# An LSTM on one Trainium2 core: one more matmul call with a zero operand in each time step

## The reference

```python
xW = einsum('ntd,dk->tnk', x, Wx) + b          # 256 -> 1024 columns
def step(h, c, xw):
    a = xw + h @ Wh                            # [4, 1024]
    i, f, o = sigmoid(a[:, 0:256]), sigmoid(a[:, 256:512]), sigmoid(a[:, 512:768])
    g = tanh(a[:, 768:1024])
    c = f * c + i * g
    h = o * tanh(c)
out = x + hs                                   # h starts as cond_1024, c as 0
```

## Time and profile before

| what | value |
|---|---|
| runs (3) | 1094.28 to 1101.48 us, median 1100.56 us |
| the profiled execution | 1090.95 us |
| its span, first to last instruction | 1089.2 us |
| mean granted clock of TensorE in it | 0.963 of full |
| busy: VectorE, TensorE, ScalarE | 790.8, 697.3, 550.4 us |

### The profile page before, as it was taken

One profiled execution on the slowest core, in us unless ns is written; L12 is line 12 of the kernel. 1 busy time (PEld: TensorE's weight loads), 2 busy tenths in 40 slices (PEclk: granted clock), 3 DMA queues, 4 the chain that ended last, 5 costly groups with the idle time before them and its releaser, 6 DMA issues.

```text
span 1089.2 us, 88137 instructions
## 1 busy us (share of the span) xinstructions
PE 697.3 (64%) x36864; PEld 574.9 (53%) x36864; DVE 790.8 (73%) x4897; ACT 550.4 (51%) x3586; POOL 0.7 (0%) x6
## 2 busy tenths in 40 slices
PE   4666666666666666666666666667666666766664
PEld 3555555555555555555555555555555555545554
DVE  4777777777777777777776777776777777777776
ACT  2455555555545555555554555554545555455554
POOL 0000000000000000000000000000000000000000
PEclk9999999999999999999998999998999998999999
DMA  3000000000000000000000000000000000000000
GB/s 89 5 7 5 6 6 6 6 6 5 7 5 6 7 5 5 6 6 6 6 6 6 5 6 7 5 6 6 6 6 6 6 6 6 5 6 6 6 6 7
DMA packets 32110, 8.74 MB, mean 8 GB/s; under 512 B 31584, under 2 KB 31584, under 8 KB 32096
## 3 DMA queue, kind: packets, MB, share of 16 engines
q1 hardware_dynamic: 31488, 8.41, 3.5%
q10 hardware_dynamic: 608, 0.14, 0.1%
HBM read 6.43 MB, written 2.10 MB: 8 GB/s over the span
## 4 chain that ended last, share of the span: by engine, by line
DVE 51%; PE 24%; ACT 14%; issue 8%; SPq 1%; DVEq 1%; DMA 0%
DVE turned_bank L296 39%; PE gates L364 24%; DVE h_pad L314 8%; ACT tanh_o L212 8%; ACT turned_bank L215 7%; DVE scan_both L301 3%; DVE cell L307 1%; DVEq L330 1%; SPq L139 1%; DVE h_rows L270 0%; DMA wh_raw<-in_L_cond_Wh_dram 0%; SPq L143 0%; DVEq L269 0%; DVE wh L225 0%; DVE wh L222 0%
## 5 line engine op out<-in xcount | busy, mean ns | idle before, releaser
L364 PE MATMUL gates<-wh,h_pad 128*32 128x64 f32 x32768 | 591.2, 227 | 374.8 <-DVE h_pad L314 373.3
L364 PEld LDWEIGHTS gates<-wh,h_pad 128*32 128x32 f32 x32768 | 506.5, 114 | 488.3 <-DVE h_pad L314 486.4
L296 DVE STREAM_TRANSPOSE turned_bank<-gates 128x64 f32<-128x64 f32 x2048 | 478.5, 262 | 182.3 <-PE gates L364 170.0
L203 ACT ACTIVATE tanh_f<-turned_bank 128x8 f32<-128x8 f32 x512 | 90.7, 177 | 438.1 <-DVE turned_bank L296 427.6
L210 ACT ACTIVATE scan_both<-turned_bank 128x8 f32<-128x8 f32 x1024 | 185.1, 181 | 59.9 <-DVE turned_bank L296 17.3
L314 DVE SCALAR_TENSOR_TENSOR h_pad<-tanh_o,turned_bank 128x4 f32<-128x4 f32 x1024 | 132.7, 158 | 74.2 <-ACT turned_bank L215 4.6
L307 DVE TENSOR_TENSOR_SCAN cell<-scan_both 128x12 f32<-128x12 f32 x1024 | 144.0, 181 | 2.1 <-issue 0.3
L215 ACT ACTIVATE turned_bank<-cell 128x4 f32<-128x4 f32 x1024 | 143.3, 172 | 2.5 <-DVE cell L307 0.3
L346 PE MATMUL x_acc<-wx,x_units 128*32 128x128 f32 x2048 | 107.5, 285 | 9.3 <-DVE x_units L249 9.3
L212 ACT ACTIVATE tanh_o<-turned_bank 128x8 f32<-128x8 f32 x512 | 90.7, 177 | 28.9 <-DVE turned_bank L296 6.7
L216 ACT ACTIVATE half_d<-cell 128x8 f32<-128x8 f32 x512 | 100.4, 196 | 0.0
(11 more groups left out here) (24 smaller groups left out, 6.7 us busy)
## 6 DMA issues: line engine op xcount, KB each, us to landing
x_next<-in_x_dram SPq DMA_DIRECT2D x256, 8.0 KB
x_here<-in_x_dram SPq DMA_DIRECT2D x256, 8.0 KB
out_dram<-y_rows SPq DMA_DIRECT2D x256, 8.0 KB
wx_raw<-in_L_cond_Wx_dram SPq DMA_DIRECT2D x8, 128.0 KB, 3.4
wh_raw<-in_L_cond_Wh_dram SPq DMA_DIRECT2D x8, 128.0 KB, 2.7
bias_raw<-in_L_cond_b_dram ACTq DMA_DIRECT2D x4, 32.0 KB, 3.1
h_rows<-in_cond_dram ACTq DMA_DIRECT2D x4, 1.0 KB
```

The costliest lines, as they stand in the source:

```text
L203: nc.scalar.activation(tanh_f[:], of_step(BF, t), ACT.Tanh).then_inc(tanh_f_done, 1)
L296: nc.vector.transpose(turned[k], gates[k][:, 0:W]).then_inc(gates_turned[k], 1)
L364: last = nc.tensor.matmul(gates[k][q * R:(q + 1) * R, 0:W], h_stationary(b, t), wh[:, b, q, columns_of(k)], start=False, stop=b == M - 1, ...
```

## The change

A function `keep_busy` on TensorE issues one call: stationary operand `zeros` (128 rows, 32 columns, all zero), moving operand the 256 columns of `wh[:, 0, 0, :]`, output partitions 0 to 31 of columns 256 to 511 of `x_acc`, which nothing reads. It uses column tile (0, 0) and accumulates (`start=False`). It is called once in each step: right behind the calls for O at t = 0 to 6 (ahead of `x_product` where there is one) and in all steps of the last chunk, and at t = 7 of the loop behind the last `inject`. It carries no wait and raises no semaphore. Two clears are added on VectorE before the loop, of `zeros` and of all 512 columns of `x_acc`, and TensorE waits for `zeroed` to reach 2 ahead of `wx_made` too.

```diff
         h_pad = sb("h_pad", [128, M, (STEPS + 1) * WIN])
+        zeros = sb("zeros", [128, R])
...
             nc.vector.memset(half_d[:], 0.0)
+            nc.vector.memset(zeros[:], 0.0)
+            nc.vector.memset(x_acc[:], 0.0)
...
+            def keep_busy():
+
+                nc.tensor.matmul(x_acc[0:R, GC:2 * GC], zeros[:], wh[:, 0, 0, :], start=False, stop=True,
+                                 tile_position=(0, 0), skip_group_check=True)
+
...
                 for k in (BA, BB, BO):
                     recur(0, k)
                     recur(1, k).then_inc(gates_done[k], 1)
+                if t < STEPS - 1 or not ahead:
+                    keep_busy()
                 if t == STEPS - 1 and ahead:
                     pe.wait_ge(x_part_made, chunk + 2)
                     for k in BANKS:
                         pe.wait_ge(gates_turned[k], now)
                         inject(k)
+                    keep_busy()
                 if ahead and 0 <= t - FIRST_PIECE_AT < len(PIECES):
                     x_product(*PIECES[t - FIRST_PIECE_AT], chunk + 1)
 
+            pe.wait_ge(zeroed, 2)
             pe.wait_ge(wx_made, M)
```

## The result

| | before | changed |
|---|---|---|
| median | 1097.42 us (4 runs, 1087.36 to 1101.48) | 1061.64 us (4 runs, 1060.75 to 1062.23) |
| ratio | | 0.9687, 95% interval 0.9615 to 0.9758 |
| profiled execution | 1090.95 us | 1062.23 us |
| span, mean granted clock | 1089.2 us, 0.963 | 1060.4 us, 0.999 |

The changed kernel is 3% faster, and the forecast of 1068.4 us is 6.8 us too high. Its direction, its range and its mechanism stand; one term of the sum is wrong.

What follows compares the result with a forecast made beforehand. The kernel was taken as one loop of waits, slowed by falls of TensorE's clock. From the profiled 1090.95 us, minus 24.5 for the falls plus 2 at t = 7, gave 1068.4 us; range 1062 to 1085 us.

Steps and rivals of the forecast that it cites:

- What bounds the kernel, and the price of the falls: A loop of waits between engines; falls of TensorE's clock to half cost 24.5 us, about 23 falls.
- Whether the call stops them: The call's 0.43 us lifts TensorE's lean stretches, so the loop's clock falls go: -24.5 us, bounds 0 and -25.3.
- rivals 1, 2 and 4: In order: clock falls as before, 1102.6 us (0.12); falls stay, call overruns, 1117 us (0.04); half go, 1081 us (0.04).
- The call at t = 0 to 6: The call lies in TensorE's idle gap of 0.91 us, or 0.70 us behind an x piece: cost 0.
- The call at t = 7: Behind the last `inject`, the call makes the next step 0.04 us late in 63 trips; taken as 2 us.
- Rival 3: TensorE's sequencer is held up at the loop's end, 7 to 13 us, about 1077 us; chance 0.09 shared with constant part.
- The median and the profiled execution: The median's 9.6 us above the profiled execution is nine more falls, which go too, so the median after is 1068.4 us.
- constant part: The 9.6 us in the median is something other than falls and stays: 1078 us; chance 0.09 shared with the sequencer.
- Before and behind the loop: Both clears, the wait for `zeroed` and the call behind the last step are hidden: 0, or 0.6 us if clears weren't.

## Why the prediction was right, and where it was wrong

- **What bounds the kernel, and the price of the falls.** Right. 23.6 us in the loop were lost to falls, and they are gone. The price from three windows, 0.68 us for 0.001 of clock, was measured as 0.69 on 23 runs (0.73 with the 12 others). One reading behind it was loose: the clock's slices are not "nines and eights from end to end" but nines with three eights, all in the second half. A nine can hide a fall; it is the windows of the trace that show them from 39.5 us on.
- **Whether the call stops them.** Right in its result, and rivals 1, 2 and 4 fall with it: the clock is 0.999, and a call with a zero stationary operand counts (its moving operand isn't zero). The falls came back without the call (clears alone) and stayed away without VectorE's clears, so it is the call. The rule of the Trainium skill ("TensorE: Matmul & The Clock Gate", Part 1) that long idle gaps cost the clock doesn't cover this kernel: the longest of TensorE's 511 waits for `h` before the change took 1.1 us, and the clock fell. What came ahead of a fall was read rightly: three more stretches of 3.4 us that end at a fall, from 36.1, 565.2 and 1036.2 us, have 1.57 us of work too. (That no fall lies behind the stretch from 135.1 is in the trace, where the clock is 1.00 up to 150.44, but not in the rows that the prediction names.) The reasoning by busy time was too cautious: I leaned on the 0.43 us of the call, and 0.11 us did the same. What it is in the call that counts stays open.
- **The call at t = 0 to 6.** Right: 0, and 0 even for two calls.
- **The call at t = 7.** Right: 16.32 against 16.29 us a trip with VectorE's instructions unchanged, and 1.4 us less in the loop without this call, so 1.4 to 2 us where I took 2. Only the call's own column tile is held, and the other tiles start on time. Rival 3 falls: the branches before and after took the same 208 ns, and the next step isn't late by its 0.11 us.
- **The median and the profiled execution.** Borne out: time follows the clock over 35 runs, and no constant part is left. That the 9.6 us between these two were falls is what this leads one to expect; the clocks of the slower runs are not on record.
- **Before and behind the loop.** This is the term that was wrong: "So both clears are hidden: 0". Their time is hidden, but they are two instructions more ahead of VectorE's loop, and that alone saves 6.4 us (1068.04 against 1061.64 us). The sum for the call was 1068.4, and the call by itself measured 1068.0; that it is so close is partly luck, since its terms were uncertain by more than that. The row to read beforehand was VectorE's own: a trip at full clock was 16.29 us where eight steps of 2.016 make 16.13, and I didn't ask what the 0.16 us were. They are 0.12 at t = 4 and 0.04 at t = 6.

## What to carry to other kernels

A chain of short steps can cost TensorE its clock with no long gap anywhere; here the longest wait was 1.1 us. A mean granted clock under 1 and trips of one loop that differ by a fixed amount show it. In this kernel a tiny call of no use in each step (some 0.11 us was enough) gave it back for almost nothing; it costs only where it reaches past the next step's start. When a change adds or removes instructions ahead of an unrolled hardware loop, the loop's own length can move, here by 0.6% with one instruction, and a comparison with a version of the same number of instructions keeps that apart from what the change itself does. And where run times scatter, plot them against the granted clock before anything else.

## What the runs showed of the hardware that I had not expected

- Matmuls on other column tiles overtake one that waits for its tile (tiles by count, as said above): six records of the x piece started at 431.90, ahead of the call's second record at 432.11 that stands before them in the program.
- One tiny instruction ahead of VectorE's loop moved the kernel from 1068.0 to 1061.5 us, and twelve moved it to 1071.1 us, in which a delay of 0.12 us in each trip went away and came back one step earlier. One, two, four, six and eight gave the same 1061 to 1063 us.
- A shorter trip can have more falls: with the clears alone a trip took 16.22 instead of 16.29 us, the clock was 0.925 to 0.970 in ten runs against 0.956 to 0.974 in 23 of the kernel before, and the kernel was not faster (ratio 1.0012).
